# A mixture of experts over sorted rows, or every chosen expert over every row

## The chip, the cores and the metric

The kernel runs on one core of a Trainium2 chip. The metric is the device time of one execution in microseconds (us). Engines are named as the profile names them: PE is the tensor engine (PEld its weight loads), DVE the vector engine, ACT the scalar engine, POOL is GpSimd, SP issues most DMAs.

## What is computed

The input is 8 sequences of 512 rows with 128 features, in float32. Six residual layers follow one another, each on layer-normalised rows: an adapter FFN, attention with 16 heads, the adapter FFN again, a mixture of experts (MoE 1), a selective scan, and the mixture of experts again (MoE 2). The mixture, cut to what matters, with H = 128, I = 512, E = 8, K = 2 and xf the 4096 normalised rows:

```python
scores = jax.nn.sigmoid(xf @ gate_w + bias)
top_scores, top_idx = jax.lax.top_k(scores, K)
top_scores = top_scores / (jnp.sum(top_scores, axis=-1, keepdims=True) + 1e-06)
w = jnp.zeros((T, E), dtype=xf.dtype).at[jnp.arange(T)[:, None], top_idx].add(top_scores)
up = jnp.einsum('th,ehi->tei', xf, up_w) + up_b
hact = jax.nn.gelu(up, approximate=False)
eo = jnp.einsum('tei,eih->teh', hact, down_w) + down_b
combined = jnp.einsum('teh,te->th', eo * 0.1, w)
shared = (jax.nn.gelu(xf @ sw_up + sb_up, approximate=False) @ sw_down + sb_down) * 0.1
out = (shared + combined).reshape(b, s, h)
out = out / (jnp.max(jnp.abs(out), axis=-1, keepdims=True) + 1e-06)
```

The layer adds half of `out` to x. `gate_w` is drawn with a deviation of 0.02 over the root of 128, and `bias` with one of 0.1. Only the two experts with the highest scores count for a row.

## The kernel before

A row tile is 128 rows, a sequence (index b or t) is four tiles, c counts them. The kernel is a row of blocks of instructions, one stream an engine, ordered by hand with semaphores. `set_up` and two weight blocks come first, then `adapter_ffn` (f1), `attention` with a loop over the sequences, `adapter_ffn` (f2), `moe_ffn` (m1), `selective_scan` and `moe_ffn` (m2). Between m1 and the scan stand two barriers and a clearing of semaphores. Each stage does work for the next one in its gaps: f2 and the scan normalise the rows for the MoE (`norm_rows` L500, `row_norm` L2346, into `mw_rows`, which holds all 32 tiles), transpose them into `xT_all` and take the gate's logits. `m1` prepares the first sequences of the scan (`scan_lead_pe`, `scan_lead_act`, `silu`, `inputs_pool`).

`moe_ffn` (L1353 on) has two parts. The shared FFN goes through the eight sequences: per sequence an up part, four products of 128x128 weights with 512 rows (L1707), four Gelus on ACT (L1525), and a down part, 16 products of 128x128 with 128 columns (L1714). ACT copies the sums to `acc` (L1548), DVE adds the bias (L1635). A float32 product shows as two records in the profile, so an up part has 8 records and a down part 32. PE does up of t, then down of t - 1.

Beside that, DVE works out in a chain of 37 dependent steps (from L1582 on) which two experts each row chose and at which place of the sorted list each row goes. POOL then scatters the rows with 64 indirect DMAs (`scatter`, L1483) of 128 rows into the DRAM tensor `sorted_rows`, in four lists of 16; the first three lists are sent before the first result is put back. The list is cut in two halves of 39 blocks of 128 rows, a fixed number that holds for any choice, so 78 blocks are computed whatever the rows chose, padded with empty rows that `fill_sorted` wrote at the kernel's start (10 MB).

The second part goes through the 78 blocks. SP loads a block's rows and its expert's up weights (256 KB) from DRAM. PE transposes the rows (L1737), does four up products (L1745) and four down products (L1754), all with 128 columns. ACT copies the transposed rows (L1532) and does four Gelus (L1539); DVE adds the bias and scales by the row's weight (L1682, L1686). POOL sends the block's results to `pair_rows` in DRAM with an indirect DMA (`put`, L1489). When the results of a half are written, SP reads them back by sequence, and DVE adds both, finds each row's largest value, scales, adds to x (`finish`, L1648 to L1662) and takes statistics (L96). The second half's four sequences come after the last block.

## Time and profile before

| | us |
|---|---|
| median of 3 runs (1555.86 to 1562.26) | 1561.59 |
| the profiled execution | 1572.32 |
| its span | 1570.2 |
| of it: up to the shared FFN of MoE 1 | 643.7 |
| MoE 1 (shared 99.4, blocks 185.9, tail 40.8) | 326.1 |
| selective scan | 293.1 |
| MoE 2 (shared 98.1, blocks 185.0, tail 24.2) | 307.3 |

The span is the time from the first to the last instruction of the profiled execution. The page gives each engine's busy time. "Idle before" is how long an engine stood still ahead of an instruction and what ended the wait: another engine's instruction, a DMA, "issue" (the profile shows nothing that it waited for), "remote" (something that the profile can't name) or the sequencer of PE ("PEq"). A stretch is a window of the span; the granted clock of PE is given as a share of full speed, 1.00 or less.

### The profile page before, as it was taken

What the parts mean: (1) busy time and instruction counts of PE and PEld (TensorE: products, weight loads), DVE (VectorE), ACT (ScalarE), POOL (GpSimd) and SP (SyncE); (2) the same over time, 40 slices, a digit from 0 to 9 for tenths busy, and PEclk for the clock granted to TensorE, in tenths of its full rate; (3) what the DMA queues carried; (4) which work ended last, traced back from release to release, by engine and by line L of the source; (5) the groups of instructions that cost most, each with busy time, mean ns of one, the idle gap of its engine ahead of it and who ended that gap; (6) DMA issues with size and microseconds to landing.
All of it is one profiled execution on the core that took longest, in us unless ns stands there. A gap on an engine that the chain in (4) does not pass through costs nothing. (4 is left out here: it accounts for less than half of the span.)

```text
span 1570.2 us, 30207 instructions
## 1 busy us (share of the span) xinstructions
PE 1286.0 (82%) x8434; PEld 725.2 (46%) x8434; DVE 964.0 (61%) x2082; ACT 827.2 (53%) x1988; POOL 676.2 (43%) x880
## 2 busy tenths in 40 slices
PE   2987999999999698884789974988998796568993
PEld 1761222222222376553689861221222254568983
DVE  5787898898898186500223744899989740023455
ACT  0221788888888434421356653666665451235661
POOL 3123223223220222474445531788788537354442
PEclk9995999999999799786899996899998888689996
DMA  5970222212220100212457742444444121346774
GB/s 116 170 155 1 72 73 82 71 43 69 71 72 22 19 16 2 59 49 83 126 159 209 223 120 77 150 155 140 150 141 147 64 71 60 97 127 177 221 212 129
DMA packets 161935, 164.76 MB, mean 105 GB/s; under 512 B 31389, under 2 KB 113771, under 8 KB 161800
## 3 DMA queue, kind: packets, MB, share of 16 engines
q1 hardware_dynamic: 150592, 145.92, 34.2%
q0 software_dynamic: 9088, 16.94, 3.1%
q8 instruction: 63, 1.03, 0.3%
q10 hardware_dynamic: 2120, 0.28, 0.1%
q14 instruction: 72, 0.59, 0.1%
HBM read 115.45 MB, written 45.90 MB: 103 GB/s over the span
## 5 line engine op out<-in xcount | busy, mean ns | idle before, releaser
L1193 DVE TENSOR_REDUCE at_nm<-at_mx 128x2 f32<-128x1024 f32 x256 | 303.9, 1220 | 40.5 <-PE at_mx L1036 39.2
L1139 ACT ACTIVATE at_probs<-at_ring 128x512 f32<-128x512 f32 x512 | 269.4, 605 | 47.4 <-PE at_ring L1048 45.8
L1539 ACT ACTIVATE m_hidden<-m_pU,mw_up_b 128x128 f32<-128x128 f32 x624 | 178.7, 371 | 127.7 <-PE m_pU L1745 70.6
L1489 POOL DMA_INDIRECT pair_rows<-m_y,m_y_id x156 | 152.5, 977 | 203.0 <-DVE m_y L1686 123.3
L1754 PE MATMUL m_pD<-m_down_all,m_hidden 128*128 x1248 | 175.9, 286 | 37.5 <-ACT m_hidden L1539 30.9
L2236 POOL TENSOR_TENSOR ss_hc<-ss_h,ss_c_all 128x512 f32<-128x512 f32 x128 | 161.7, 1270 | 52.3 <-DVE ss_h L2406 45.5
L1745 PE MATMUL m_pU<-m_hidden,m_up_now 128*128 128x128 f32 x1248 | 174.4, 285 | 7.3 <-issue 6.5
L1754 PEld LDWEIGHTS m_pD<-m_down_all,m_hidden 128*128 128x128 f32 x1248 | 158.9, 199 | 43.7 <-issue 42.9
L1048 PE MATMUL at_ring<-at_qq,at_kk 51*128 51x512 bf16 x512 | 163.3, 386 | 7.1 <-ACT at_probs L1139 6.1
L1036 PE MATMUL at_mx<-at_kk,at_qq 48*128 48x512 bf16 x512 | 156.0, 399 | 13.1 <-DVE at_nm L1193 8.0
L1745 PEld LDWEIGHTS m_pU<-m_hidden,m_up_now 128*128 128x128 f32 x1248 | 160.6, 201 | 9.6 <-issue 9.6
L2406 DVE TENSOR_TENSOR_SCAN ss_h<-ss_pA,ss_beta 128x512 f32<-128x512 f32 x128 | 155.2, 1215 | 13.8 <-issue 6.1
L1483 POOL DMA_INDIRECT sorted_rows<-mw_rows,m_index x128 | 126.2, 986 | 57.3 <-issue 40.4
L1060 PE MATMUL at_po<-at_probs,at_va 128*32 128x512 f32 x1024 | 138.1, 612 | 0.1
L1682 DVE TENSOR_TENSOR m_yt<-m_pD,mw_down_b 128x128 f32<-128x128 f32 x156 | 45.4, 291 | 147.3 <-PE m_pD L1754 74.8
L2271 PE MATMUL ss_pY<-ss_hc,ss_total 128*32 128x512 f32 x256 | 125.7, 640 | 11.8 <-POOL ss_hc L2236 11.8
L2371 ACT ACTIVATE ss_pA<-ss_dtb,ss_a_neg 128x512 f32<-128x512 f32 x128 | 87.4, 684 | 44.4 <-DVE ss_h L2406 44.4
L1714 PE MATMUL m_pD<-m_down,m_hidden 128*128 128x128 f32 x512 | 72.2, 293 | 42.6 <-issue 42.5
L728 POOL CAST at_nmp<-at_nm 128x16 bf16<-128x16 f32 x32 | 6.3, 197 | 228.9 <-DVE at_nm L1193 228.9
L1635 DVE TENSOR_TENSOR m_xT_all<-m_xT_all,m_down_b 128x512 f32<-128x512 f32 x16 | 11.0, 690 | 146.9 <-ACT m_xT_all L1548 135.6
L2427 DVE TENSOR_TENSOR ss_beta<-ss_pX,ss_b_all 128x512 f32<-128x512 f32 x128 | 85.1, 670 | 13.4 <-PE ss_pX L2256 13.4
L1714 PEld LDWEIGHTS m_pD<-m_down,m_hidden 128*128 128x128 f32 x512 | 68.0, 208 | 54.5 <-issue 54.4
(319 smaller groups left out, 1948.7 us busy)
## 6 DMA issues: line engine op xcount, KB each, us to landing
m_up_now<-in_L_ffn_up_w_dram SPq DMA_DIRECT2D x156, 256.0 KB
ss_dtb<-ss_dt_rows SPq DMA_DIRECT2D x128, 256.0 KB
sorted_rows<-empty_row SPq DMA_DIRECT2D x2, 5070.0 KB, 47.2
m_xb<-sorted_rows SPq DMA_DIRECT2D x156, 65.0 KB
m_hidden<-pair_rows SPq DMA_DIRECT2D x32, 256.0 KB
at_qq<-q_stack SPq DMA_DIRECT2D x64, 96.0 KB, 2.2
at_kk<-k_stack SPq DMA_DIRECT2D x64, 96.0 KB, 2.3
m_down_all<-in_L_ffn_down_w_dram SPq DMA_DIRECT2D x16, 256.0 KB, 4.3
```

The costliest lines, as they stand in the source:

```text
L1036: last = pe.matmul(mx[parity][:, c, :], qq[rows(parity, STACK), pair, q_at:q_at + P], kk[rows(parity, STACK), pair, :], start=True, stop=True)
L1048: pe.matmul(ring[bank][:, :], kk[rows(h, STACK + 3), h // 2, tile * P:(tile + 1) * P], qq[rows(h, STACK + 3), h // 2, :], start=True, stop ...
L1060: last = pe.matmul(po[VW * h4:VW * (h4 + 1), :], va[:, tile, group * GH + h4, :], probs[:, (slot % 2) * GH + h4, :], start=(tile == 0), st ...
L1139: act.activation(probs[:, (slot % 2) * GH + ORDER[j], :], ring[bank][:, :], ACT.Exp, scale=SCALE).then_inc(s.exp_done, 1)
L1193: dve.tensor_reduce(nm[group % 2][:, 2 * (pair % 2) + parity, 2 * half:2 * half + 2], mx[parity][:, :, :], AX.X, ALU.max, negate=True).the ...
L1489: pool.indirect_dma_start(pair_rows, bass.IndirectOffsetOnAxis(ap=y_id[j % Y_BUFS][:, :], axis=0), y[j % Y_BUFS][:, :], None, bounds_check ...
L1539: act.activation(hid[j % T_BUFS][:, k, :], pU[j % 2][:, k * P:(k + 1) * P], ACT.Gelu, bias=v.up_b[:, bass.ds(e, 1), k:k + 1].rearrange("p ...
L1714: last = pe.matmul(pD[t % 2][:, c, :], hidden[t % 2][:, k, c * P:(c + 1) * P], m.down[:, k, :], start=(k == 0), stop=(k == NI - 1))
L1745: last = pe.matmul(pU[j % 2][:, k * P:(k + 1) * P], up_now[j % U_BUFS][:, k * P:(k + 1) * P], xT[j % T_BUFS], start=True, stop=True)
L1754: last = pe.matmul(pD[j % 2][:, 0, :], hid[j % T_BUFS][:, k, :], down_all[:, bass.ds(e, 1), k, :].rearrange("i a d -> i (a d)"), start=(k ...
L2236: pool.tensor_tensor(hc[m % HC_RING][:, :], h[m % HC_RING][:, :], c_all[old % 2][:, :], ALU.mult).then_inc(y.hc, 1)
L2406: dve.tensor_tensor_scan(h[m % HC_RING][:, :], pA[m % A_RING][:, :], beta[m % B_RING][:, :], 0.0, ALU.mult, ALU.add).then_inc(y.h, 1)
```

## The change

The sorting goes, and with it everything between the rows and the experts: the places, the scatters, `sorted_rows`, `pair_rows`, the empty rows, the constants for them and the loads of all the experts' weights in advance. In its place:

- DVE works out in a chain of 31 steps, with a count product on PE before the third up part (`COUNT_AT`), a weight of every row for every expert (0 where the row didn't choose it), a list of the experts with those ahead that some row chose, and from their number the trips of a loop: 1 for up to four experts, 2 for up to six, else 3.
- Every engine then runs `listed_experts`: two experts a trip and two behind the loop. An expert is a full pass over the eight sequences, with the products of the shared FFN; weights are in two sets of buffers, and SP loads the set of the expert after next when it is free. DVE adds the bias to the down part's result and adds it into `acc`, scaled by the row's weight from a column that is addressed by a register. In the last pass `finish` follows for each sequence.
- The scan's first inputs are made within the last pass, by sequence; the elementwise products of them that DVE made (`inputs_pool`) go to POOL.
- `norm_rows` and `row_norm` write to one tile of a sequence instead of `mw_rows` and wait until PE has transposed the sequence before.
- The barriers and the clearing of semaphores between m1 and the scan go.
- f1, f2 and attention lose the empty row, the fill, the constants and the bias loads. The order of their products stays as it is.

The core of the diff ("..." where lines are left out):

```diff
+                if b > 0:
+                    act.wait_ge(rows.s.xT_done, b)
+                scale_rows(act, g, rows.t, b, rows_xn).then_inc(rows.s.xn_ready, 1)
...
+COUNT_AT = 2
...
-def fill_sorted(sp, r):
-    sp.wait_ge(r.made, 2)
-    for rows in r.sorted:
-        sp.dma_start(rows.rearrange("(j p) d -> p j d", p=P), r.empty[:, :].unsqueeze(1).broadcast_to([P, TB, ROW])
-                     ).then_inc(r.filled, 16)
...
-def make_moe_constants(pool, v):
-    small = dict(allow_small_or_imprecise_dtypes=True)
-    pool.iota(v.ramp[:, :], pattern=[[-1, E1]], base=E1, channel_multiplier=0, **small).then_inc(v.made, 1)
...
-def moe_ffn(nc, g, v, m, ins, dram, sem, tag, ahead=None, lead=None, spare=None, out=None):
-
-    s = m.s
-    sorted_rows, pair_rows = dram
...
+            def listed_experts(eng, expert):
+                eng.wait_ge(s.list_ready, 1)
+                trips = eng.value_load(pairs[0:1, 0:1], min_val=1, max_val=E1 // 2 - 1)
+                with eng.Fori(0, trips) as i:
+                    expert(2 * i + 1, 1, 2 * i, i, False)
+                    expert(2 * i + 2, 0, 2 * i + 1, i, False)
+                expert(2 * trips + 1, 1, 2 * trips, trips, False)
+                expert(2 * trips + 2, 0, 2 * trips + 1, trips, True)
+            @block.sync
+            def _(sp):
+                def expert(n, buf, place, trip, is_last):
+                    e = sp.value_load(listed[0:1, bass.ds(place, 1)], min_val=0, max_val=E1 - 1)
+                    sp.wait_ge(s.down_done, NB * n - NB + 2)
+                    sp.dma_start(up[buf][:, :], ins["L1_ffn_up_w"][e]).then_inc(load_in[buf], 16)
+                    sp.dma_start(down[buf][:, :, :], ins["L1_ffn_down_w"][e].rearrange("(k i) h -> i k h", i=P)
+                                 ).then_inc(load_in[buf], 16)
+                    sp.dma_start(up_b[buf][:, :], ins["L1_ffn_up_b"][e].rearrange("(k i) -> i k", i=P),
+                                 allow_slow_non_contiguous=True).then_inc(load_in[buf], 16)
+                    sp.dma_start(down_b[buf][:, :], row_to_all(ins["L1_ffn_down_b"][e])).then_inc(load_in[buf], 16)
+                listed_experts(sp, expert)
+                if lead is not None:
+                    scan_lead_stores(sp, lead)
+                if out is not None:
+                    for b in range(NB):
+                        sp.wait_ge(s.x_done, b + 1)
+                        sp.dma_start(out[b].rearrange("(c p) d -> p c d", p=P), g.X[:, b]).then_inc(s.x_out, 16)
...
+                pool.iota(ramp[:, :], pattern=[[-1, E1]], base=E1, channel_multiplier=0,
+                          allow_small_or_imprecise_dtypes=True).then_inc(s.fin, 1)
+                pool.wait_ge(s.fin, 1)
+                pool.iota(index[:, :], pattern=[[1, E1]], base=0, channel_multiplier=0,
+                          allow_small_or_imprecise_dtypes=True).then_inc(s.fin, 1)
+                pool.wait_ge(s.fin, 2)
+                pool.iota(limits[:, :], pattern=[[2, 2]], base=4, channel_multiplier=0,
+                          allow_small_or_imprecise_dtypes=True).then_inc(s.fin, 1)
+                if ahead is not None:
+                    make_scan_constants(pool, g, ahead)
+                if lead is not None:
+                    zero_columns(pool, lead)
+                    take_shift(pool, g, lead, slice(0, 1), 0)
+                    take_shift(pool, g, lead, slice(1, 2), 1)
+                    for n in range(NS):
+                        inputs_pool(pool, lead, 0, n)
...
+                def expert(n, buf, place, trip, is_last):
+                    for t in range(NB):
+                        gelus(n, buf, t)
+                        if is_last and lead is not None:
+                            scan_lead_act(act, g, q=ahead, s=lead, t=t)
+                listed_experts(act, expert)
...
+                link(dve.reciprocal(den[:, :], den[:, :]))
+                link(dve.tensor_tensor(w8[:, :, :], sig[:, :, :], wide(den), ALU.mult))
+                link(dve.tensor_reduce(count[:, :], hot[0][:, :, :].rearrange("p t e -> p e t"), AX.X, ALU.add))
+                dve.wait_ge(s.counted, 1)
+                link(dve.tensor_scalar(key[:, :], pC[:, 0:E1], 0.0, -float(E1), ALU.is_gt, ALU.mult))
+                link(dve.tensor_reduce(pairsf[:, :], key[0:1, :], AX.X, ALU.add))
+                link(dve.tensor_scalar(pairsf[:, :], pairsf[:, :], -1.0 / E1, None, ALU.mult))
+                link(dve.tensor_tensor(more[:, :], limits[:, :], pairsf[:, :].broadcast_to([1, 2]), ALU.is_lt))
+                link(dve.tensor_reduce(pairsf[:, :], more[:, :], AX.X, ALU.add))
+                link(dve.tensor_scalar(pairs[:, :], pairsf[:, :], 1.0, None, ALU.add))
...
+                chain.end()
+                dve.tensor_copy(listed[:, :], listf[:, :]).then_inc(s.list_ready, 1)
+                for r in range(E1):
...
+                for half in range(2):
+                    dve.sem_inc(pD_free[half], 1)
...
+                def expert(n, buf, place, trip, is_last):
+                    dve.wait_ge(load_in[buf], LOADS * (trip + 2 - buf))
+                    for t in range(NB):
+                        if is_last and lead is not None and t == 4:
+                            silu(dve, lead, 0)
+                        dve.wait_ge(s.down_done, NB * n + t + 1)
+                        dve.tensor_tensor(out_b[t % 2][:, :, :], pD[t % 2][:, :, :],
+                                          down_b[buf][:, :].unsqueeze(1).broadcast_to([P, NC, D]), ALU.add
+                                          ).then_inc(pD_free[t % 2], 1)
+                        dve.wait_ge(pD_free[t % 2], NB // 2 * n - NB // 2 + t // 2 + 2)
+                        for c in range(NC):
+                            at = acc[:, t * NC + c, :]
+                            last = dve.scalar_tensor_tensor(
+                                out=at, in0=out_b[t % 2][:, c, :],
+                                scalar=w_listed[:, t * NC + c, bass.ds(place, 1)], in1=at,
+                                op0=ALU.mult, op1=ALU.add)
+                        if is_last:
+                            last.then_inc(s.acc_done, 1)
+                            dve.wait_ge(s.acc_done, t + 1)
+                            finish(t)
+                listed_experts(dve, expert)
...
+                    if t == COUNT_AT:
+                        pe.wait_ge(s.step, 18)
+                        pe.matmul(pC[:, 0:E1], g.onesf[:, :], count[:, :], start=True, stop=True).then_inc(s.counted, 1)
+                    if t < NB:
+                        up_product(0, 0, t)
...
+                def expert(n, buf, place, trip, is_last):
+                    pe.wait_ge(load_in[buf], LOADS * (trip + 2 - buf))
+                    for t in range(NB + 1):
+                        if t < NB:
+                            up_product(n, buf, t)
+                        if t == 1:
+                            pe.wait_ge(s.shared_acc, NB)
+                        if is_last and lead is not None:
+                            scan_lead_pe(pe, g, q=ahead, s=lead, t=t)
+                        if t > 0:
+                            pe.wait_ge(pD_free[(t - 1) % 2], NB // 2 * n - NB // 2 + (t - 1) // 2 + 1)
+                            down_product(n, buf, t - 1)
+                listed_experts(pe, expert)
...
             def row_norm(b, half):
                 if half == 0:
                     act.wait_ge(r.shifted, lot_of(b) + 1)
+                    if b > 0:
+                        act.wait_ge(r.xT_done, b)
                 for c in (2 * half, 2 * half + 1):
-                    last = act.activation(v.rows[:, b * NC + c, 0:D], g.X[:, b, c, :], ACT.Identity, bias=row_shift[:, b, c:c + 1],
+                    last = act.activation(rows[:, c, :], g.X[:, b, c, :], ACT.Identity, bias=row_shift[:, b, c:c + 1],
```

## Rows read from the trace of the kernel before

**Rows 1.** The page: the span, and the share of the tensor engine.
```profile
span 1570.2 us, 30207 instructions
PE 1286.0 (82%) x8434; PEld 725.2 (46%) x8434; DVE 964.0 (61%) x2082; ACT 827.2 (53%) x1988; POOL 676.2 (43%) x880
```

**Rows 2.** Table of stretches; after the length: busy (x instructions) by engine, clock, DMA.
```profile
643.70:743.10 99.40, 72.71 (x324) 48.42 (x325) 23.44 (x49) 28.59 (x43) 58.47 (x71) 0.79 0.26 75
743.10:929.00 185.90, 162.44 (x1326) 157.82 (x1326) 74.42 (x307) 104.39 (x394) 93.49 (x98) 0.94 0.59 168
929.00:969.80 40.80, 11.94 (x27) 3.92 (x27) 23.56 (x70) 14.49 (x24) 1.51 (x2) 0.71 0.23 68
...
1262.90:1361.00 98.10, 70.70 (x325) 47.50 (x326) 21.45 (x49) 28.69 (x43) 49.39 (x53) 0.81 0.27 76
1361.00:1546.00 185.00, 161.70 (x1326) 157.51 (x1326) 70.30 (x274) 102.52 (x390) 89.76 (x93) 0.94 0.61 175
1546.00:1570.20 24.20, 0.00 (x0) 0.00 (x0) 14.64 (x40) 0.00 (x0) 0.93 (x1) 0.51 0.42 130
```

**Rows 3.** Timeline of PE, shared FFN: start, duration, engine, line, tiles, records.
```profile
643.72 9.66 PE L1707 MATMUL m_pU<-m_xT_all,m_up 128*128 128x512 f32 x16 [0.53 <-PEq L305]
...
658.63 3.60 PE L1707 MATMUL m_pU<-m_xT_all,m_up 128*128 128x512 f32 x8
662.07 3.73 PE L1714 MATMUL m_pD<-m_down,m_hidden 128*128 128x128 f32 x32
665.64 3.60 PE L1707 MATMUL m_pU<-m_xT_all,m_up 128*128 128x512 f32 x8
...
1262.94 8.96 PE L1707 MATMUL m_pU<-m_xT_all,m_up 128*128 128x512 f32 x16 [0.53 <-PEq L2117]
```

**Rows 4.** Timeline, PE and ACT, later in them; POOL's scatters (one of two stretches).
```profile
720.09 0.37 PE L1714 MATMUL m_pD<-m_down,m_hidden 128*128 128x128 f32 x1 [2.43 <-issue]
...
1304.04 0.59 ACT L1548 COPY m_xT_all<-m_pD 128x512 f32<-128x512 f32 x1 [8.01 <-remote]
...
643.70:743.10 99.40, 48.48 (x49) 0.79 0.26 75
```

**Rows 5.** Groups by line: ACT's Gelu, DVE's bias add and scaled add.
```profile
L1525 ACT ACTIVATE m_hidden<-m_pU,m_up_b 128x512 f32<-128x512 f32 x64 | 42.6, 689 | 15.7 <-PE m_pU L1707 7.3 <-DMA at_qq<-at_ms 6.9 <-issue 1.2
...
L1662 DVE SCALAR_TENSOR_TENSOR X<-m_xT_all,m_most,X 128x128 f32<-128x128 f32 x64 | 18.2, 347 | 0.3
...
L1635 DVE TENSOR_TENSOR m_xT_all<-m_xT_all,m_down_b 128x512 f32<-128x512 f32 x16 | 11.0, 690 | 146.9 <-ACT m_xT_all L1548 135.6 <-issue 11.4
```

**Rows 6.** Timeline of PE in attention's loop: the regular pause, one of five alike.
```profile
233.40 0.63 PE L1014 MATMUL at_ring<-identf,at_xn 128*128 128x128 f32 x4 [1.03 <-DVE at_ao L1175]
```

**Rows 7.** Timeline of DVE: first and last step of one sequence's normalisation.
```profile
937.61 0.69 DVE L1654 TENSOR_REDUCE m_most<-m_xT_all 128x4 f32<-128x512 f32 x1
...
940.19 0.86 DVE L96 BATCH_NORM_STATS2 bn<-X 128x6 f32<-128x128 f32 x4
```

**Rows 8.** Groups by line: the scan's inputs on POOL and ACT.
```profile
L1924 POOL TENSOR_TENSOR ss_nd<-ss_wm,ss_edt 128x512 f32<-128x512 f32 x7 | 8.9, 1270 | 0.0
...
L2033 ACT ACTIVATE ss_edt<-ss_zy,ss_b_dtp 128x512 f32<-128x512 f32 x8 | 5.5, 685 | 3.8 <-PE ss_zy L1986 3.8
```

**Rows 9.** Timeline of DVE: the scan stage's first instruction, and the last one.
```profile
969.79 0.20 DVE L104 TENSOR_TENSOR mean<-bn 128x24 f32<-128x24 f32 x1 [8.21 <-PEq L2491]
...
1566.31 1.14 DVE L1662 SCALAR_TENSOR_TENSOR X<-m_xT_all,m_most,X 128x128 f32<-128x128 f32 x4
```

**Rows 10.** Timeline of PE and ACT at the end of the second adapter stage.
```profile
629.23 0.60 PE L394 MATMUL f_pR<-identf,mw_rows 128*128 128x128 f32 x4
...
629.50 1.65 ACT L154 ACTIVATE mw_rows<-X,m_rows_shift,rstd 128x128 f32<-128x128 f32 x4 [2.30 <-POOL m_rows_shift L147]
```

**Rows 11.** Table of stretches: two adapter steps of f1 beside the fill, two of f2.
```profile
56.10:74.25 18.15, 17.55 (x234) 13.71 (x234) 15.59 (x58) 7.02 (x19) 2.91 (x10) 1.00 1.25 172
551.30:569.45 18.15, 17.53 (x233) 13.69 (x234) 14.80 (x56) 5.14 (x14) 2.27 (x8) 1.00 0.08 28
```

More of the change, by code:

```diff
@@ L153, in scale_rows @@
     for c in range(NC):
[L154 removed]
+        last = act.activation(out[:, c, :], g.X[:, b, c, :], ACT.Identity, bias=t.shift[:, b, c:c + 1],
                               scale=g.rstd[:, b, c:c + 1])
@@ L1665, in finish @@
                     last.then_inc(s.x_done, 1)
-                if piece == 4 and out is None:
-                    last = take_stats(dve, g, b, s.x_done, b + 1)
+                    if out is None:
+                        last = take_stats(dve, g, b, s.x_done, b + 1)
                     if lead is not None and b < 2:
```

623 lines of the change are left out of this document (163 added, 460 removed).

## The prediction

> **What bounds the kernel now.** I read the page first, for the span and the busy shares [rows 1], then a table of stretches that cuts the two expert stages (MoE 1 and MoE 2) out of the span [rows 2]. Each has three parts. The shared FFN takes 99.4 us in MoE 1 and 98.1 us in MoE 2, with the tensor engine (PE) busy for only 72.7 and 70.7 us of it. The 78 sorted blocks take 185.9 and 185.0 us, with PE busy 87%. Then comes a tail almost without PE: 40.8 us (results read back, normalisation, scan inputs) and 24.2 us (results, normalisation, store). From 643.7 to 969.8 that is 326.1 us, from 1262.9 to the end 307.3 us. The change touches little outside these stretches.
>
> What a dense pass costs is in the timeline of PE in the shared FFN [rows 3]. At the full granted clock one sequence of 512 rows is an up part of 3.44 us (658.63 to 662.07) and a down part of 3.57 us (662.07 to 665.64): 7.01 us, 56.1 us for eight. The expert passes of the changed kernel issue just these products at these shapes. Why does the shared FFN then take 98 us and not 59? Later in the same stretch PE issues one product, idles 2.43 us, issues the next, with nothing waited for but "issue", and ScalarE (ACT) sits idle 8.01 us for "remote" [rows 4]. Meanwhile GpSimd (POOL) issues its indirect scatters, 49 in this stretch and in its twin [rows 4]. In MoE 1 the pauses begin after the first scatters and stop when POOL is done with 48 of them, the first three of its four lists. I read them as the scatters keeping the engines from getting their instructions or events. About 39 us in each stage stand on that reading.
>
> **Part by part.** *How many passes.* The new list keeps only experts that some row chose; the trip count makes it 4, 6 or 8 passes. The gate's weights give logits a spread of 0.02, its drawn biases are 0.048, -0.002, -0.023, -0.017, 0.099, 0.124, 0.054, -0.009. Evaluating the reference on its own inputs, the 8192 choices fall as 122, 0, 0, 0, 3937, 3969, 164, 0 in the first stage and 142, 0, 0, 0, 3908, 3916, 226, 0 in the second. Four experts are used, so the loop makes one trip (2 passes) and 2 more follow: 4 dense passes and the shared one. In 128-row units that is 128 against 78 blocks; a block is cheap for its rows only where it isn't stalled.
>
> *Shared FFN without scatters.* The first two up parts run at a cold clock: 9.5 us in MoE 1, 8.96 us in MoE 2 [rows 3]. Then 8 down parts of 3.57 and 6 up parts of 3.44 us, 49.2 us, and 0.3 us for the one small count product: 59.0 and 58.5 us. The chain on the vector engine (DVE) before the count is 18 short steps, some 9 us; PE comes to the count after 12.5 us, so nothing waits.
>
> *Expert passes.* PE 7.01 us per sequence. ACT does 4 Gelus of 0.689 us, 2.8 us. DVE does one bias add of 128x512 (0.690 us) and four multiply-adds (0.347 us each), 2.1 us, some 2.6 with gaps [rows 5]. Both stay under PE. Weights (0.5 MB a pass) are asked for some 40 us ahead. 4 x 56.1 = 224.4 us. No row shows the loop's start, its exit and waits on registers in this place. The nearest are attention's loop, where the longest regular pause of PE in an iteration is 1.03 us and is put down to DVE [rows 6], and at the other end the 8.01 us of ACT. I take 1.5 us a stage, near the first, since PE's queue runs ahead here too. The range starts at 0: a gain is excluded, as the 56.1 us already hold PE without a pause.
>
> *Tail of MoE 1.* The scan's first inputs move from the tail into the last expert pass. On PE before the last up part ends they add 5.2 us (three convolution products and two projections at 0.86, two transposes); then come lift and the second convolution (3.5 us), down 6 and down 7. From its start, the last pass reaches the end of down 7 at 64.8 us. DVE then does the last accumulation (2.4 us) and the normalisation and statistics, 3.44 us from start to end [rows 7], and ends at 71.1. Beside it run ACT's exponentials (0.685 us each, and a table load) and six products on POOL, now at 1.27 us each [rows 8], that DVE had made: these end at 67.3, and their 12 stack stores are issued by 71.9 us. With 0.3 for the block change: 72.2 us. The two barriers and the semaphore clearing, part of DVE's 8.21 us of idle ahead of 969.79 [rows 9], go. In the last pass DVE has 6.1 us of work per 7.01, so it is the engine next to the bound.
>
> *Tail of MoE 2.* Accumulation 2.6 and normalisation 2.6 after the last down part, then the store: before, the last result was ready at 1567.45 and the span ended 2.75 us later [rows 9]. 8.0 us in place of 24.2.
>
> *The rest.* The rows buffer of the second adapter stage becomes one tile, so ACT's normalisation of sequence 6 waits for the transposes of 5 (start 629.23, about 1.1 us long) and starts at 630.3 in place of 629.50 [rows 10]; the sequence's copy, logits and the products behind them wait in ACT's order: +0.8 us. In the scan the same wait is met, since the transposes are issued a step earlier. The 10 MB fill at the start, the empty row, the constants on POOL and nine bias loads on SP go; two adapter steps take the same 18.15 us and the same PE time beside the fill and without it [rows 11], so I count 0. Despite the change's name, the order of the Gram blocks and base products isn't touched.
>
> *Sum.* MoE 1: 59.0 + 3 x 56.1 + 72.2 + 1.5 + 0.8 = 301.8, for 326.1: -24.3. MoE 2: 58.5 + 224.4 + 1.5 + 8.0 = 292.4, for 307.3: -14.9. Together -39.2 on a span of 1570.2 us, whose execution took 1572.3: 1533. The median of the runs, 1561.6, lies 10.7 us below that execution. Either the 10.7 are spread over all, and the median becomes 1522; or profiling had lengthened the scatter stretches that vanish, and it becomes 1533. (They can't be profiling altogether: they are 78 us, the difference is 10.7.) I take **1527 us**, -2.2%.
>
> **A rule against the change.** The loop body is long and a jump may cost. The pauses in [rows 4] already show that an engine can be left without instructions for 2.43 or 8.01 us. The Trainium skill (Runtime: NRT & Kernel Launch, "Instruction fetch mechanics") says that a taken branch to code outside the fetched window stops the engine until it is fetched, and that kernels had better be unrolled; by that rule this is the jump rival below. The same section says that crossing to the next piece of straight code is mostly hidden: the pauses in the shared FFN, which is straight code, disagree.
>
> **The rivals.**
> - *The pauses belong to PE's own stream of instructions, not to the scatters* (slower). They begin in both stages after the same products, some 37 us into the stage, which fits a place in the code as well as it fits the scatters. Then they stay, 39 us a stage: 1527 + 78 = 1605 us. It decides as soon as half of them stays. Against: the sorted blocks issue more instructions per us and run at 87% [rows 2]; the scatters end as the pauses do. 7%.
> - *More passes* (slower). One pair at a fifth expert makes 6: + 4 x 56.1 = 1751 us. Against: the counts above, where no second-rank logit comes near. 3%.
> - *Jumps refill the engines.* At 8.01 us for loop start and exit in each stage, 32 - 3 us more: 1556 us, no measurable change. Attention's loop speaks against. 9%.
> [...]
> - *More gain*: the tail of MoE 1 hides better, or the scan's start gains from weights already there: down to 1508. 6%.
>
> **How the numbers follow.** Forecast with the DVE variant 75%: 1515 to 1545, from the loops at 0 to 5 us a stage and the two readings of the 10.7 us. To reach 8 in 10 the range takes in the gain case and the jumps: 1508 to 1560. A measurement of this kernel can tell about 0.5% from no change, here 1553.8 to 1569.4. Faster: 75 + 6 + a third of the jumps, 84%. Same: the rest of the jumps, 6%. Slower: 10%.
>
> **What would show it.** Right: no indirect DMA, 640 up and 2560 down records for the ten passes, seven us a sequence in every pass, a shared pass of 59 us, MoE 1 near 302 and MoE 2 near 292 us, the granted clock at 1.0 through them, PE idle only in some 8 us behind each stage. Wrong: pauses of 1.4 to 2.4 us behind "issue" in the shared pass; gaps where passes change; more than four expert passes; a last pass with PE waiting for DVE.

## The result and the profile after

The changed kernel takes 1535.6 us (median of four runs, 1530.8 to 1536.4), the kernel before, timed again beside it, 1558.7 us (1554.5 to 1562.3): a ratio of 0.9845, 95% interval 0.9818 to 0.9872, 1.5% faster. The forecast was 1527 us and 2.2%. Profiled execution against profiled execution it is 1536.1 us against 1572.3; the profile of the kernel before isn't one of its four timed runs. On two other chips, however, the kernel before takes 1456 and 1458 us. The changed kernel as it stands wasn't run on those two, but a variant of it whose edit gained nothing (e8) took 5.4% more than the kernel before on one of them. The experiments show which stretches of the kernel before differ, and that is the main thing to learn from this case; what differs in the chips they don't show.

The page of the changed kernel, to be laid beside [rows 1]: the span, the busy shares, and the granted clock of PE in 40 slices.

```profile
span 1534.3 us, 24908 instructions
PE 1386.0 (90%) x8338; PEld 725.6 (47%) x8338; DVE 946.8 (62%) x1898; ACT 800.9 (52%) x1465; POOL 400.0 (26%) x585
...
PEclk9995899999999989699999997899999979999999
```

The table of stretches, in the columns of [rows 2]: shared FFN, three expert passes, the last pass with its tail, the scan, and the whole of MoE 2.

```profile
645.28:704.13 58.85, 58.85 (x323) 41.98 (x324) 23.01 (x49) 29.03 (x42) 9.21 (x21) 0.96 0.05 11
704.13:872.30 168.17, 168.17 (x963) 122.26 (x962) 43.01 (x116) 66.54 (x97) 0.00 (x0) 1.00 0.05 12
872.30:947.55 75.25, 65.61 (x349) 44.26 (x347) 46.92 (x165) 39.19 (x61) 10.41 (x12) 0.95 0.03 10
947.55:1243.20 295.65, 259.05 (x710) 67.02 (x711) 250.38 (x353) 174.36 (x315) 224.42 (x191) 0.88 0.40 132
1243.20:1534.00 290.80, 282.92 (x1602) 204.85 (x1602) 98.00 (x274) 117.58 (x171) 0.40 (x3) 0.99 0.06 16
```

The first number behind the length is PE's busy time: in the shared FFN and in three expert passes PE is busy for the whole of it (58.85 and 168.17 us), where [rows 2] had 26.7 us of idle time in the shared FFN alone. MoE 1 takes 302.3 us (326.1 before) and MoE 2 291.1 (307.3). The timeline of PE, in the columns of [rows 3], shows that a change of pass costs it nothing:

```profile
645.28 9.61 PE L1531 MATMUL m_pU<-m_xT_all,m_up 128*128 128x512 f32 x16 [0.53 <-PEq L305]
...
704.13 4.46 PE L1531 MATMUL m_pU<-m_xT_all,m_up 128*128 128x512 f32 x10
...
760.18 5.32 PE L1531 MATMUL m_pU<-m_xT_all,m_up 128*128 128x512 f32 x12
...
816.23 6.17 PE L1531 MATMUL m_pU<-m_xT_all,m_up 128*128 128x512 f32 x14
...
872.29 6.17 PE L1531 MATMUL m_pU<-m_xT_all,m_up 128*128 128x512 f32 x14
```

The four passes begin 56.05 us apart (8 x 7.01), with no bracket of idle time behind them, at the loop's entry, inside its body and at its exit alike.

### The profile page after: what moved, and what is told of

The parts are those of the page before. It is cut to its first block and busy times, and to the rows that moved or that the text cites. A ratio compares the mean times of both kernels' runs of the same rounds, so it can differ in the third digit from the quotient of the medians.

```text
span 1534.3 us, 24908 instructions
## 1 busy us (share of the span) xinstructions
PE 1386.0 (90%) x8338; PEld 725.6 (47%) x8338; DVE 946.8 (62%) x1898; ACT 800.9 (52%) x1465; POOL 400.0 (26%) x585
## 5 line engine op out<-in xcount | busy, mean ns | idle before, releaser
L1382 ACT ACTIVATE m_hidden<-m_pU,m_up_b 128x512 f32<-128x512 f32 x320 | 219.8, 687 | 265.6 <-PE m_pU L1531 265.3
L1538 PEld LDWEIGHTS m_pD<-m_down,m_hidden 128*128 128x128 f32 x2560 | 296.7, 192 | 32.5 <-issue 32.5
L1538 PE MATMUL m_pD<-m_down,m_hidden 128*128 128x128 f32 x2560 | 297.1, 275 | 0.0
L1531 PE MATMUL m_pU<-m_xT_all,m_up 128*128 128x512 f32 x640 | 291.2, 601 | 1.1 <-PEq L305 0.5
L1507 DVE TENSOR_TENSOR m_out_b<-m_pD,m_down_b 128x512 f32<-128x512 f32 x64 | 44.3, 692 | 288.3 <-PE m_pD L1538 288.3
L1531 PEld LDWEIGHTS m_pU<-m_xT_all,m_up 128*128 128x128 f32 x640 | 118.0, 193 | 123.7 <-issue 123.5
L1033 PEld LDWEIGHTS at_mx<-at_kk,at_qq 48*128 48x128 bf16 x512 | 33.6, 95 | 125.1 <-DVE at_nm L1190 71.0
L1513 DVE SCALAR_TENSOR_TENSOR m_acc<-m_out_b,m_w_listed,m_acc 128x128 f32<-128x128 f32 x256 | 74.1, 352 | 9.3 <-DVE m_out_b L1507 2.1
L1045 PEld LDWEIGHTS at_ring<-at_qq,at_kk 51*128 51x128 bf16 x512 | 35.9, 94 | 53.2 <-ACT at_probs L1136 41.4
L2050 PEld LDWEIGHTS ss_pX<-ss_stack,ss_spread 96*128 96x128 bf16 x128 | 12.7, 101 | 100.5 <-DVE ss_beta L2223 57.0
```

The costliest lines, as they stand in the source:

```text
L1033: last = pe.matmul(mx[parity][:, c, :], qq[rows(parity, STACK), pair, q_at:q_at + P], kk[rows(parity, STACK), pair, :], start=True, stop=True)
L1045: pe.matmul(ring[bank][:, :], kk[rows(h, STACK + 3), h // 2, tile * P:(tile + 1) * P], qq[rows(h, STACK + 3), h // 2, :], start=True, stop ...
L1382: act.activation(hidden[t % 2][:, k, :], pU[k][:, :], ACT.Gelu, bias=up_b[buf][:, k:k + 1]).then_inc(s.gelu_done, 1)
L1531: pe.matmul(pU[k][:, :], up[buf][:, k * P:(k + 1) * P], xT_all[:, t, :], start=True, stop=True).then_inc(s.up_done, 1)
L1538: last = pe.matmul(pD[t % 2][:, c, :], hidden[t % 2][:, k, c * P:(c + 1) * P], down[buf][:, k, :], start=(k == 0), stop=(k == NI - 1))
```

## The experiments

The theory at the start was that of the prediction: GpSimd's scatters make the pauses. Its rivals were that they belong to a place in PE's instructions, that jumps cost something that the four passes don't show, and that profiling had lengthened the first profile. The kernel before was timed beside every group of runs, and that turned out to be the most telling number:

| runs | chip | kernel before, us | PE's pauses in it |
|---|---|---|---|
| the result | not known | 1559 (4 runs) | yes [rows 4], in a fifth execution |
| e1 to e4 | A | 1457.7 (7 runs) | none |
| e5 | B | 1570.1 (7 runs) | not profiled |
| e6 to e8 | C | 1456.3 (7 runs) | not profiled |
| e9 | D | 1562.8 (1 run) | not profiled |
| e10; e11 and e12 | E | 1564.2; 1567.5 (1 run each) | yes (e12, its second stage) |

A to E are five different chips by their numbers on record. E was met twice and behaved alike both times, each other chip once, so a property of the chip isn't told apart from one of the session or of the place of the program in memory.

**e1: the kernel before, profiled again.** No edit.

> The kernel before, unchanged, profiled a second time. Its first profiled execution took 1572.3 us, 13.6 us above the median of its four timed runs (1558.7); the changed kernel's profiled execution took 1536.1 us against a median of 1535.6. Theory: profiling lengthens the shared FFN stretches beside the scatters, which the changed kernel has no longer. Then this profile shows again about 1572 us, with 99 and 98 us for the two shared FFNs. Rival: the first profile was one long execution. Then this one takes about 1559 us, and the two shared FFNs together some 14 us less (or the scan, the attention stage or a tail is shorter). The scan took 293.2 us before and 295.7 us in the changed kernel: if it moves by 2 us or more between two profiles of one kernel, the 2.5 us are no effect of the change.

It took 1458.0 us: 114 us less than its first profile. Neither theory had that in reach. Its table of stretches, cut at the same events as [rows 2]:

```profile
644.80:711.50 66.70, 61.06 (x325) 42.76 (x325) 23.46 (x50) 29.65 (x43) 44.54 (x55) 0.93 0.22 66
711.50:873.30 161.80, 154.31 (x1326) 151.10 (x1326) 75.55 (x306) 103.82 (x394) 108.18 (x114) 0.98 0.74 212
873.30:914.50 41.20, 11.56 (x27) 3.77 (x27) 23.66 (x70) 14.70 (x25) 1.72 (x2) 0.74 0.21 68
1206.80:1272.10 65.30, 59.96 (x324) 42.34 (x324) 21.43 (x49) 29.59 (x43) 35.21 (x37) 0.97 0.23 68
1272.10:1430.20 158.10, 152.43 (x1326) 150.47 (x1326) 70.28 (x272) 102.03 (x390) 104.01 (x109) 0.98 0.78 224
1430.20:1455.80 25.60, 0.00 (x0) 0.00 (x0) 15.28 (x42) 0.00 (x0) 1.73 (x2) 0.54 0.39 123
```

The same program, the same scatters at the same 1.28 us beside the same products, and PE has no idle time behind "issue" in either stage: 32.7 and 32.8 us less in the shared FFNs, 24.1 and 26.9 less in the blocks, nothing less in the tails. The 114 us lie wholly where indirect DMAs run. Not all of it is pauses: of the 32.7 us some 21 are idle time, and 11.7 are PE's products, which took 61.06 us in place of 72.71, at a granted clock of 0.93 in place of 0.79. So the scatters alone don't make pauses, and the block stretches of [rows 2] were stretched too. On this chip a stage of the kernel before takes 269.7 and 249.0 us, for 302 and 291 of the changed one.

**e2 and e7: the scatters behind the shared FFN.** One wait in GpSimd's program of the kernel before:

```diff
             pool.wait_ge(s.placed, 1)
+            pool.wait_ge(s.shared_acc, NB)
             for t in range(HT):
```

> The kernel before, with GpSimd's 64 indirect scatters of each stage held back until the shared FFN is over. Theory (the scatters make the pauses): the shared FFN takes 59 us in the first stage and 58.5 us in the second, without a pause behind issue; then PE waits for the first 32 scatters (32 x 1.28 us, about 42 us, plus the first loads, 46 in all), and the first blocks run beside 32 more scatters as a part did before; in all 1559 - 39 x 2 + 46 x 2 = 1573 us, 1560 to 1595. Rival (the pauses belong to a place in PE's stream of instructions): the shared FFN stays at 98 us in each stage, and the time rises by 92 us to about 1650 us.

> The kernel before with its scatters behind the shared FFN once more, the same as e2_scatters_late, which took 1546 us on a chip on which the kernel before takes 1458. Theory, where the kernel before takes 1555 to 1575 us beside it: the shared FFN takes 59 us without a pause, and the pauses move to the blocks, which then run beside the second 32 scatters; 1565 to 1640 us. Rival (place in the code): pauses stay in the shared FFN and it takes 98 us a stage, about 1650 us. Where the kernel before takes 1458 us: 1546 us.

1546.4 us (four runs, ratio 1.061, 1.058 to 1.063) and 1546.9, both on chips where the kernel before has no pauses. PE then waits 48.3 us for the first rows, which are 32 scatters. As tests of the pauses both are void: there were none to move, and e2's two forecasts (1573 and 1650 us) both started from 98 us a shared FFN.

**e3 and e6: 48 scatters added to each stage of the changed kernel.** They start when the list of experts is ready and write rows to a tensor that nobody reads.

```diff
+                pool.wait_ge(s.list_ready, 1)
+                for t in range(SCATTERS):
+                    pool.indirect_dma_start(away, bass.IndirectOffsetOnAxis(ap=away_at[:, t:t + 1], axis=0),
+                                            xT_all[:, t // 8, 0:132], None, bounds_check=SCATTERS * P - 1,
+                                            oob_is_err=False).then_inc(away_out, 16)
+                    if t % 16 == 15:
+                        pool.wait_ge(away_out, 16 * (t + 1))
```

> The changed kernel with 48 indirect scatters of 128 rows x 528 bytes added to each MoE stage on GpSimd, started when the list of experts is ready, into a DRAM tensor that nobody reads; in lists of 16 with a wait behind each. They run some 17 us into the stage for about 66 us, over the rest of the shared pass and the first expert pass. Theory (the scatters make the pauses): PE pauses of 1.4 to 2.4 us behind issue come back in that stretch, some 30 to 40 us a stage, so the time is 1600 to 1615 us. Rival (place in the code): no pause, 1536 us; GpSimd's own work fits behind them, so nothing else should move by more than 2 us.

> The changed kernel with the 48 added scatters of each stage once more, the same as e3_scatters_added, where PE showed no pause beside them (shared FFN 58.8 us, first expert pass 56.1) on a chip on which the kernel before takes 1458 us. Theory (pauses need a chip of the other kind and scatters beside PE's work): where the kernel before takes 1555 to 1575 us beside it, the pauses of 1.4 to 2.4 us behind issue show in this kernel, 30 to 40 us a stage, and it takes 1600 to 1615 us. Rival (on such a chip the kernel before pauses for another cause, its code or its other traffic): 1542 us there too. Where the kernel before takes 1458 us beside it, both say 1542 us.

1542.1 and 1535.9 us on chips A and C: no pause, 302.2 and 290.9 us for the stages of e3. (The 6 us between the two are the scan's, 302.7 and 297.0 us.) They say only that on such a chip 48 scatters cost nothing, and they serve as the reference for e9 to e11.

**e4: six expert passes.** The loop makes two trips; the fifth and sixth pass have weights of zero.

```diff
-                pool.iota(limits[:, :], pattern=[[2, 2]], base=4, channel_multiplier=0,
+                pool.iota(limits[:, :], pattern=[[2, 2]], base=2, channel_multiplier=0,
```

> The changed kernel with the loop making two trips in place of one, so six expert passes in place of four, the last two with weights of zero. It takes the back jump that four passes never take. If a jump costs PE nothing, each stage grows by 2 x 56.05 = 112.1 us and the time is 1535.6 + 224.2 = 1760 us, with the passes of one stage beginning 56.05 us apart. If the back jump refills the engines at about 8 us, the distance across the jump is 64 us and the time 1776 us.

1757.2 us. The two stages in the table of stretches:

```profile
644.80:1059.20 414.40, 404.76 (x2269) 290.03 (x2269) 142.25 (x410) 178.85 (x264) 19.67 (x33) 0.99 0.04 11
1352.70:1755.50 402.80, 394.66 (x2242) 286.25 (x2242) 127.31 (x354) 161.57 (x235) 0.40 (x3) 0.99 0.06 15
```

PE's timeline at two pass starts; the loop's body is two passes, so the jump back lies ahead of 815.77:

```profile
759.72 4.46 PE L1531 MATMUL m_pU<-m_xT_all,m_up 128*128 128x512 f32 x10
...
815.77 4.46 PE L1531 MATMUL m_pU<-m_xT_all,m_up 128*128 128x512 f32 x10
```

The stages grew by 112.1 and 111.7 us, and the start behind the jump comes 56.05 us after the one before it: this jump costs PE nothing. The changed kernel's time also follows the draw: 112 us a stage for each pair of experts more.

**e5: the changed kernel again.**

> The changed kernel, unchanged, timed against the kernel before beside it. With the last four experiments the kernel before took 1457.7 us (7 runs, 1455 to 1461) in place of 1558.7 us: the same scatters ran beside the shared FFN, but its PE showed no pause behind issue. Theory: the pauses are a property of where the program ran (chip, or place of its memory), not of the scatters alone; the changed kernel has no pauses at either place, so it stays at 1535 us, and the ratio depends on the place: 0.985 where the kernel before pauses, about 1.053 where it does not. Rival: the chip of those experiments is faster in all things, then there the changed kernel falls to about 1436 us and the ratio stays 0.985.

1534.7 us (four runs, 1532.3 to 1535.9) for 1570.1 of the kernel before: 0.977, interval 0.972 to 0.982. The changed kernel takes the same time to 1 us as in the result, while the kernel before takes 11 us more. The forecast "1535 at either place" got its other half from e8.

**e8: the convolution of sequence 1 behind down part 6.** In the last pass of MoE 1 of the changed kernel:

```diff
         lift(pe, q, s, 0)
+    if t == 8:
         for k in range(3):
             convolve(pe, q, s, 1, k)
```

> The changed kernel with the three convolution products of sequence 1 behind the down part of sequence 6 in the last expert pass of the first stage, in place of ahead of it. In the profile of the changed kernel that down part ends only 3.5 us ahead of the last one, and DVE needs 5.4 us a sequence, 7.4 beside GpSimd's products, so DVE ends 75.0 us after the pass began where 71.1 were predicted. Theory: DVE starts on sequence 6 2.6 us sooner, the last pass takes 72.7 us up to the start of the scan in place of 75.3, and the time is 1532 us (ratio to the changed kernel 0.998, less than three rounds can tell; the stretch in the trace decides). Rival: the last stack stores, behind ScalarE and GpSimd, end the stage, and less than 1 us is gained. DVE's four scaled adds of a sequence take 1.14 us alone and 2.07 to 2.12 us while GpSimd runs products: that should now hit other instructions of DVE, for the same number of microseconds on GpSimd.

1534.6 us (four runs) on a chip where the kernel before takes 1456.3: a ratio of 1.054 (1.052 to 1.056). Since this edit gained nothing, as the next lines show, it stands for the changed kernel on a chip without pauses. From the last pass's start (871.13) to the scan's (946.29) it is 75.2 us, for 75.3: the gain of 2.6 us did not come. DVE began on sequence 6 at 930.64, 59.5 us into the pass in place of 62.1, but:

```profile
930.64 0.69 DVE L1507 TENSOR_TENSOR m_out_b<-m_pD,m_down_b 128x512 f32<-128x512 f32 x1 [2.79 <-PE m_pD L1538]
931.48 4.14 DVE L1513 SCALAR_TENSOR_TENSOR m_acc<-m_out_b,m_w_listed,m_acc 128x128 f32<-128x128 f32 x4 [0.15 <-DVE m_out_b L1507]
...
937.58 2.07 DVE L1490 SCALAR_TENSOR_TENSOR X<-m_acc,m_most,X 128x128 f32<-128x128 f32 x4
```

In the changed kernel the same two steps were 2.12 and 2.07 us, and where GpSimd is idle 1.14 each:

```profile
934.37 0.69 DVE L1507 TENSOR_TENSOR m_out_b<-m_pD,m_down_b 128x512 f32<-128x512 f32 x1 [5.36 <-PE m_pD L1538]
935.22 2.12 DVE L1513 SCALAR_TENSOR_TENSOR m_acc<-m_out_b,m_w_listed,m_acc 128x128 f32<-128x128 f32 x4 [0.15 <-DVE m_out_b L1507]
937.37 0.69 DVE L1482 TENSOR_REDUCE m_most<-m_acc 128x4 f32<-128x512 f32 x1
...
938.83 2.07 DVE L1490 SCALAR_TENSOR_TENSOR X<-m_acc,m_most,X 128x128 f32<-128x128 f32 x4
...
942.62 1.14 DVE L1513 SCALAR_TENSOR_TENSOR m_acc<-m_out_b,m_w_listed,m_acc 128x128 f32<-128x128 f32 x4 [0.15 <-DVE m_out_b L1507]
```

Moved earlier, DVE's scaled adds met three of GpSimd's products back to back and lost 3.0 us to them in place of 1.0. From its start on sequence 6 to its start on sequence 7 (940.53) DVE took 9.9 us in place of 7.4, which uses up 2.5 of the 2.6 us. The reduction (one input) and the bias add (one input in PSUM) keep their 0.69 us. The Trainium skill (SBUF — State Buffer, "SBUF: two separate sides") states this: a DVE operation with two SBUF inputs and a GpSimd operation that reads SBUF exclude each other for a whole instruction. The two traces agree, with the 1.0 and 3.0 us above.

**e9: scatters in the first stage, plain stores in the second.** e3's kernel, with 48 plain stores of the same 128 x 528 bytes from GpSimd in MoE 2.

```diff
+                        pool.dma_start(away[t * P:(t + 1) * P, :], xT_all[:, t // 8, 0:132]).then_inc(away_out, 16)
```

> The changed kernel with 48 indirect scatters added beside the first stage's shared pass and first expert pass (as in e3_scatters_added), and 48 plain stores of the same 128 x 528 bytes, issued by GpSimd too, at the same place of the second stage. The kernel before has been met at about 1457 us on two chips and at 1559 to 1570 us on others. Where it takes 1457 us beside this run: no pause in either stage, 1535 to 1542 us. Where it takes 1555 to 1575 us: if the indirect scatters make the pauses on such a chip, PE pauses of 1.4 to 2.4 us show in the first stage, 30 to 40 us; if any flow of stores does, they show in both stages, 1600 us and more; if the cause lies in the code of the kernel before, in neither, 1535 to 1542 us.

1562.3 us on chip D, where the kernel before takes 1562.8. The two stages in the table of stretches:

```profile
644.10:976.40 332.30, 305.16 (x1629) 214.67 (x1629) 110.86 (x330) 134.07 (x200) 70.62 (x82) 0.95 0.07 20
1269.70:1560.50 290.80, 282.71 (x1602) 204.76 (x1602) 97.94 (x274) 117.54 (x171) 26.19 (x52) 0.99 0.10 28
```

PE's timeline in the first:

```profile
674.79 3.51 PE L1556 MATMUL m_pD<-m_down,m_hidden 128*128 128x128 f32 x30
678.71 0.40 PE L1556 MATMUL m_pD<-m_down,m_hidden 128*128 128x128 f32 x2 [0.41 <-issue]
...
705.84 0.81 PE L1556 MATMUL m_pD<-m_down,m_hidden 128*128 128x128 f32 x3 [1.73 <-issue]
...
731.61 8.41 PE L1549 MATMUL m_pU<-m_xT_all,m_up 128*128 128x512 f32 x16 [0.85 <-issue]
```

This is [rows 4] put back into a kernel that had lost it: 30.1 us more than e3's 302.2, from 678.7 (17 us behind the first scatter) to 731.6 (the last one is issued at 728.4), and not a pause behind it. Of the 30.1 us, 12.6 are PE's products running longer (305.16 us busy for 292.58 in e3). The plain stores go through the same queue with as many packets and bytes (1536 and 3.25 MB in either stretch), at 0.6 us from one to the next, twice as dense, and MoE 2 takes 290.8 us. In this one execution it is the indirect form that goes with the pauses, not the traffic. And the place in PE's instructions is out: the second stage runs the same products without a pause, and so does the first in e10 and e11 below.

**e10: scatters further apart.** e3's kernel; in the first stage GpSimd clears a scratch tile after each scatter, in the second they stay back to back.

```diff
+                    if lead is not None:
+                        pool.memset(pace[:, :], 0.0).then_inc(paced, 1)
+                        pool.wait_ge(paced, t + 1)
```

> The changed kernel with 48 scatters added to each stage, as in e3_scatters_added; in the first stage GpSimd clears a scratch tile of 128 x 1536 after each, so that they follow each other at some 2.8 us in place of 1.28; in the second stage they follow back to back. In e9_scatters_and_stores PE's pauses began only 17 us after the first scatter, behind some 13 of them, which looks like a backlog. Where the kernel before takes 1555 to 1575 us beside this run: if a backlog makes the pauses, the first stage has none (302 us) and the second has 30 to 40 us of them (about 321 to 331 in place of 291); if each scatter costs PE its share (30 us for 48, 0.6 us each), both stages are longer by about 30 us. Where the kernel before takes 1457 us: no pause in either.

**e11: two further distances.** A tile of 256 columns in place of 1536, and in the second stage only after every other scatter.

```diff
-                    if lead is not None:
+                    if lead is not None or t % 2 == 1:
```

> The changed kernel with 48 scatters added to each stage at two further paces: in the first stage GpSimd clears a small tile after each scatter (about 2.0 us from one to the next), in the second after every other (about 1.65 us on average). In e10_paced_scatters a pace of 3.15 us made no pause and 1.28 us made 36 us of them. In the blocks of the kernel before, where it pauses, scatters and results' stores alternate at 1.28 us and a block takes some 3 us, while later blocks, with results' stores alone at some 1.9 us, take 1.9 us and show no pause. Where the kernel before takes 1555 to 1575 us beside this run: a backlog that empties at one indirect DMA per 1.3 to 1.9 us says that 2.0 us makes no pause (first stage 302 us), and that 1.65 makes fewer than 36 us or none (second stage 291 to 310). If each scatter below some distance costs its share whatever the backlog, 1.65 us makes nearly the 36 us. Where the kernel before takes 1457 us: no pause.

1566.5 and 1533.5 us, on a chip where the kernel before takes 1564 to 1568. The two stages of e10 in the table of stretches:

```profile
643.60:945.90 302.30, 292.67 (x1629) 208.56 (x1629) 110.89 (x330) 134.82 (x200) 136.50 (x130) 0.98 0.08 22
1238.00:1564.80 326.80, 297.97 (x1602) 214.33 (x1602) 97.95 (x274) 116.76 (x171) 49.70 (x52) 0.94 0.08 25
```

and of e11:

```profile
646.20:948.50 302.30, 292.69 (x1629) 208.53 (x1629) 110.94 (x330) 134.78 (x200) 85.10 (x130) 0.98 0.07 22
1240.60:1531.70 291.10, 282.98 (x1602) 204.91 (x1602) 97.95 (x274) 117.58 (x171) 57.09 (x76) 0.99 0.10 27
```

| distance (first to last start of 48, over 47) | stage | its length, us | without scatters |
|---|---|---|---|
| 3.2 us (e10) | MoE 1 | 302.3 | 302.3 |
| 2.2 us (e11) | MoE 1 | 302.3 | 302.3 |
| 1.8 us (e11, 1.3 and 2.1 by turns) | MoE 2 | 291.1 | 291.1 |
| 1.4 us (e10, back to back, 1.28 inside a list) | MoE 2 | 326.8 | 291.1 |

The same 48 scatters cost 35.7 us or nothing, and what was changed is their distance (the clearing of a tile that makes it is work on GpSimd alone). Each row is one execution. Of the 35.7, 15.0 are PE's products themselves, which run longer (297.97 busy for 282.98; the clock of the stretch fell from 0.99 to 0.94), 20.7 are idle time. That each scatter costs its share is out, even of those that follow another at 1.3 us, every other one in MoE 2 of e11. A backlog that drains at one indirect DMA in something between 1.28 and 1.8 us fits, with the 17 us that pass before the first pause in e9; what fills up was not seen.

**e12: the kernel before with late scatters in its first stage only.**

```diff
             pool.wait_ge(s.placed, 1)
+            if lead is not None:
+                pool.wait_ge(s.shared_acc, NB)
```

> The kernel before with the scatters behind the shared FFN in the first stage only (as in e2_scatters_late), and the second stage as it was. Where the kernel before takes 1555 to 1575 us beside this run: if the scatters make the pauses, the first stage's shared FFN takes 59 us and the second's 98 us in the same execution, the first blocks then wait for 32 scatters, and the 16 blocks beside the scatters and results' stores take some 3 us each. If the pauses belong to a place in PE's instructions, both shared FFNs take 98 us. Where the kernel before takes 1457 us: the shared FFNs take 59 to 61 us in both, and the time is about 1500 us.

1603.8 us on the chip of e10 and e11. Shared FFN, wait and blocks of the first stage, then the shared FFN of the second:

```profile
644.30:705.20 60.90, 60.79 (x324) 42.65 (x324) 22.45 (x48) 29.09 (x43) 9.36 (x19) 0.96 0.13 35
705.20:753.00 47.80, 0.00 (x0) 0.00 (x0) 0.69 (x1) 0.56 (x1) 33.73 (x36) 0.53 0.14 48
753.00:954.20 201.20, 165.09 (x1326) 159.75 (x1326) 74.42 (x306) 104.18 (x394) 108.03 (x115) 0.90 0.61 171
...
1294.70:1391.50 96.80, 70.52 (x324) 47.74 (x324) 20.74 (x48) 28.07 (x42) 49.48 (x53) 0.79 0.26 77
```

In one execution, 60.9 us without scatters and 96.8 us beside them, in the code of the kernel before: without the scatters the shared FFN has no pauses. And the 201.2 us of blocks, for 161.8 in e1, show where the lost time went: with the scatters.

## Why the prediction was right, and where not

*What bounded the kernel.* The reading that carried most, that 39 us of each shared FFN hang on the scatters and not on PE's code, holds: e9 and e10 put the pauses back with scatters alone, and e12 takes them away with the scatters, all on chips where the kernel before takes 1563 to 1568 us. What it lacked is the condition. "I read them as the scatters keeping the engines from getting their instructions or events" took one profile of one chip for the kernel. By the time of the kernel before, five of the seven sets of runs, on three chips or more, have the pauses and two sets, on two chips, have none; there the sorted stages are 33 and 42 us shorter than the dense ones. That the measured gain came out near the forecast is therefore in part luck: it hung on which kind of chip the two kernels were timed on. The changed kernel's own time doesn't hang on it; it is 1534.6 to 1535.6 us in three sets of four runs, the third with e8's edit. Nor did a row show the engines without instructions, as the prediction has it of the pauses in [rows 4]: they show idle time whose cause the profile doesn't name. The rival with 7% for "slower" had the right question (what if the pauses don't follow the scatters' removal?) and the wrong mechanism; that they might be no property of the kernel stood nowhere. The stall share was also misplaced: of the 39 us only 33 go without the pauses (e1 keeps 66.7 us, some 6 of them a wait for the first rows), a third of these 33 are slower products and not pauses, and 24 to 27 more lay in the blocks. That did no harm to the sum, which was made of the new kernel's own terms.

*The terms.* Shared FFN 59.0, measured 58.85. Passes of 56.1, measured 56.05. The granted clock was 0.95 to 1.00 in these stretches, where 1.0 was expected. The DVE variant that the forecast's 75% takes in rests on a price for a weight column read by a register. No run shows one: the multiply-adds took 0.352 us each for 0.347 [rows 5], and the kernel before already had a DVE operation that finds an operand by a register, and it took what its neighbour took:

```profile
L1682 DVE TENSOR_TENSOR m_yt<-m_pD,mw_down_b x156: 279/292/293, 748.7 to 1544.5; 128x128 f32<-128x128 f32 x156
L1686 DVE TENSOR_SCALAR m_y<-m_yt,m_xb x156: 285/286/541, 749.1 to 1544.8; 128x128 f32<-128x128 f32 x156
```

(The first finds its bias by a register, the second finds nothing that way; shortest, median and longest in ns.) Loop and jumps 1.5 us a stage, measured 0: the 8.01 us of ACT [rows 4], which held up the upper end and the jump rival (1556), lie beside the scatters; without pauses (e1) ACT's longest wait in that stretch is 4.7 us. They told nothing of jumps. The Trainium skill's rule (Runtime: NRT & Kernel Launch, "Instruction fetch mechanics") that a taken branch to code outside the fetched window stops the engine was named beside that rival; in e4 the jump back over a body of two passes leaves the starts 56.05 us apart. So either it is hidden from PE here or its target lay inside the window; no trace tells which. The second adapter stage's +0.8 us can't be told: over all profiles MoE 1 begins between 642.6 and 646.2 us, in kernels of both kinds.

*Tail of MoE 1.* Predicted 72.2 us, measured 75.3: the step that failed is "so it is the engine next to the bound", with a mean load of 6.1 us per 7.01. Down part 7 ended at 65.6 (64.8 predicted). But the convolution products ahead of down part 6 bring the last two down parts to 3.5 us of each other, DVE needs 5.4 a sequence, so it began on the last one 1.9 us late, and the two slowed steps added 2.0; it ended at 75.0 us where 71.1 were predicted. (The prediction's own terms put DVE's end at 64.8 + 2.4 + 3.44 = 70.6 us, not 71.1; its sum goes by the stores' 71.9, so nothing hangs on it.) The products moved to GpSimd were priced at 1.27 us for the right time of GpSimd; what they take from DVE was not priced. GpSimd's chain itself was right (67.9 for 67.3; last store issued at 72.4 for 71.9). MoE 1 came to 302.3 for 301.8, MoE 2 to 291.1 for 292.4 (tail 8.3 for 8.0).

*The scan* took 295.7 us, 2.5 more than before, which I had at 0. The change didn't do that: of the two scans, that of the kernel before took 292.3 (e1) and 303.5 (e2), that of the changed kernel 292.6 (e5), 293.5 (e4), 295.7 (e8) and 302.7 (e3). The two longest have the lowest granted clock in the stretch, 0.86 for 0.88 to 0.90.

*From the sum to the median.* The sum gave an execution of 1533, the profiled one took 1536.1. The two readings of the 10.7 us gave 1522 or 1533 for the median, and I took 1527; it is 1535.6, so the second fits better: the excess of that profile belonged to stretches that vanished. Not to profiling as such, though: e1's profile (1458.0) sits on its median (1457.7). Where it pauses, the kernel before varies by itself (1567 to 1583 with e5), the changed one by 3.6 us there and 5.6 with the result.

## What to carry to other kernels

Time the kernel before on more than one chip before a stall is booked as gain: here a stall of 114 us was there on some chips and not on others, and the same change is 1.5 to 2.3% faster on those and, by e8, 5.4% slower on one of the others. Where GpSimd issues indirect DMAs back to back beside a busy tensor engine, put other work of GpSimd between them: at 1.8 us apart on average there was no pause here. Plain stores needed no such care. And an engine at 6.1 of 7.01 us keeps up only if its work arrives evenly and its neighbour doesn't hold it up (1.0 to 3.0 us here): look at the spacing of the last two arrivals, not at the mean.

## What was not expected of the hardware

That one program shows pauses of up to 2.4 us at PE on some chips and none on others, with the same instructions. They were seen in profiles from chips D and E and in the first one; of B the time alone (1570 us) says so; A and C had none. On the chips with pauses, GpSimd's indirect DMAs 1.28 us apart made them, after some 13 of them; at 1.8 us on average, none, and the results' stores of the first profile, 1.9 us apart from 832 to 866 us, ran beside a PE without a pause. Neither the cause in the chip nor what fills up is settled.

One thing in the traces points at the recording itself: the profile of the kernel before without pauses (e1) holds 23438 records of semaphore updates, that with pauses 17905, of the same 30207 instructions, and "remote" in [rows 4] may be such a missing record. Counted in the traces, a DMA of 128 rows leaves 16 records of its landing, so 48 of them leave 768:

| 48 DMAs, PE busy | distance, us | chip | records of 768 | pauses |
|---|---|---|---|---|
| indirect (e3, e6; both stages) | 1.4 | A, C | 768 | no |
| indirect (e9 MoE 1; e10 MoE 2) | 1.4 | D; E | 186; 186 | yes |
| indirect (e11 MoE 2) | 1.8 | E | 529 | no |
| indirect (e11 MoE 1) | 2.2 | E | 716 | no |
| indirect (e10 MoE 1) | 3.2 | E | 768 | no |
| plain (e9 MoE 2) | 0.6 | D | 768 | no |

So the loss of records follows the distance as the pauses do, but it sets in earlier: at 2.2 us already, and in e9 with the first scatters, 13 us ahead of the first pause (35 records up to 678.7 us, 160 in e3). And it goes with PE's work: in e12 the first two lists of 16, sent while PE stood idle, left 256 and 201 of 256 records, the third, sent beside the blocks, 23. Whether the recording makes the pauses, or both come from one cause, isn't shown. The Trainium skill (NOTIFIC — Programmer's Manual, "When the ring fills") says that a queue of records can be set to drop records or to stall the engine; no run here shows how they are set. Every timed execution on record has a span and a granted clock beside it, so no time here is known to be free of recording. If recording takes part, kernels run without it might not pause at all, and the change would be a loss there. That wasn't tried and stays open, as does whether a sorted kernel with its scatters and results' stores 1.8 us apart (142 a stage, some 256 us) would beat the dense one on the chips that pause.
